# Routed expert tiles: row transposes between the tail down matmuls, half of the tail's low part made earlier, and one weight low part made on GpSimd

## The reference, cut to what matters

```
h = _rmsnorm(x, rms_weight);  topv, topi = top_k(softmax(h @ router_w), 2)
g = einsum('td,edf->tef', ht, w_gate);  u = einsum('td,edf->tef', ht, w_up)
eo = einsum('tef,efd->ted', silu(g) * u, w_down)      # 8 experts, 1024 -> 512 -> 1024
moe = einsum('te,ted->td', w_dense, eo)               # two experts per token
sh = silu(ht @ sw_gate) * (ht @ sw_up) @ sw_down      # shared expert, all tokens
```

## Time and profile before

| what | value |
|---|---|
| median of three runs | 635.94 us |
| span of the profiled execution | 633.0 us |
| TensorE matmul busy | 611.9 us (97%) |
| DVE busy | 524.0 us (83%) |
| ACT busy | 421.6 us (67%) |
| POOL busy | 148.1 us (23%) |
| one routed tile, transposes to transposes | 26.87 us |
| mean granted clock of TensorE | 0.998 |

### The profile page before, as it was taken

The page is one execution under the profiler, slowest core; times in us unless marked ns, Lnnn a source line. Parts: engine busy times, 40 slices in busy tenths (PEclk is TensorE's granted clock), DMA queues, the critical chain, the costliest instruction groups (busy, mean ns, idle before and its releaser), DMA issues.

```text
span 633.0 us, 10577 instructions
## 1 busy us (share of the span) xinstructions
PE 611.9 (97%) x3624; PEld 475.4 (75%) x3625; DVE 524.0 (83%) x886; ACT 421.6 (67%) x558; POOL 148.1 (23%) x167
## 2 busy tenths in 40 slices
PE   8899999998999999999989999999999999999996
PEld 6678888887886444444557888898988989889775
DVE  5888888878787777889999479789797988979686
ACT  4998888889755989784574366639376483855630
POOL 2354446416000333527920310000000000000051
PEclk9999999999999999999999999999999999999999
DMA  8977776765246997936999558796775968759257
GB/s 337 420 291 298 301 303 238 310 267 191 100 174 260 403 362 286 400 134 241 402 364 416 216 204 325 262 370 224 299 315 200 390 210 319 273 219 393 86 176 264
DMA packets 31070, 177.91 MB, mean 281 GB/s; under 512 B 4064, under 2 KB 4064, under 8 KB 14784
## 3 DMA queue, kind: packets, MB, share of 16 engines
q1 hardware_dynamic: 25536, 158.64, 65.3%
q0 software_dynamic: 5504, 18.88, 8.2%
HBM read 154.30 MB, written 23.20 MB: 280 GB/s over the span
## 4 chain that ended last, share of the span: by engine, by line
PE 50%; DVE 19%; ACT 14%; issue 8%; DMA 5%; POOL 2%; DVEq 1%; POOLq 0%; ACTq 0%; SPq 0%
PE BK L2132 10%; PE BK L306 9%; DVE WL L1029 4%; ACT RA L1383 4%; ACT PR L1410 4%; PE BK L2135 3%; PE BK L1882 3%; PE BK L312 3%; PE BK L318 3%; PE BK L313 3%; DMA RA<-wbit 2%; PE BK L2102 2%; PE BK L1827 2%; DMA RX<-wbit 1%; PE BK L2155 1%
## 5 line engine op out<-in xcount | busy, mean ns | idle before, releaser
L2132 PE MATMUL BK<-EX,WH 128*128 128x320 f32 x384 | 101.3, 344 | 0.3
L1029 DVE TENSOR_TENSOR WL<-RA,WH 128x2048 fp32r<-128x2048 f32 x40 | 89.4, 2287 | 7.6 <-ACT WH L1586 7.4
L2135 PE MATMUL BK<-EX,WL 128*128 128x160 f32 x336 | 79.3, 236 | 0.0
L1586 ACT ACTIVATE WH<-RA 128x2048 fp32r<-128x2048 f32 x40 | 73.6, 1910 | 0.2 <-PE BK L1925 0.2
L2132 PEld LDWEIGHTS BK<-EX,WH 128*128 128x128 f32 x384 | 69.7, 188 | 1.9 <-DVE SR L1069 1.9
L2135 PEld LDWEIGHTS BK<-EX,WL 128*128 128x128 f32 x336 | 64.1, 191 | 0.0
L705 POOL DMA_INDIRECT GA<-rows,SLOT x4 | 4.9, 1229 | 240.4 <-DVE WL L1029 239.5
L652 POOL TENSOR_TENSOR HB<-HB,ND (+2 forms) x26 | 28.6, 1121 | 100.5 <-DVE BH L915 99.9
L1482 ACT ACTIVATE RA<-RA,RT 128x2048 int16<-128x2048 f32 x22 | 43.7, 1998 | 3.8 <-DMA RA<-wbit 1.9
L1029 DVE TENSOR_TENSOR WL<-RC,WH 128x2048 fp32r<-128x2048 f32 x20 | 45.0, 2285 | 0.7 <-ACT WH L1586 0.7
L1882 PE MATMUL BK<-TG,XQ 128*128 128x512 bf16 x192 | 42.4, 379 | 0.1
(11 more groups left out here) (328 smaller groups left out, 1644.1 us busy)
## 6 DMA issues: line engine op xcount, KB each, us to landing
RA<-wbit SPq DMA_DIRECT2D x54, 1024.0 KB, 6.7
RA<-wmoe SPq DMA_DIRECT2D x40, 1024.0 KB, 6.5
RC<-wmoe SPq DMA_DIRECT2D x20, 1024.0 KB, 8.0
rows<-ZERO POOLq DMA_DIRECT2D x40, 256.0 KB, 8.2
XG<-rows SPq DMA_DIRECT2D x10, 512.0 KB, 3.7
rows<-YS SPq DMA_DIRECT2D x9, 512.0 KB, 6.0
RA<-wqk SPq DMA_DIRECT2D x7, 640.0 KB, 7.8
RA<-wo SPq DMA_DIRECT2D x4, 1024.0 KB, 7.5
```

Source lines behind the costliest of these rows:

```text
L1029: e.tensor_tensor(WL[m][:, q * RAW:q * RAW + RAW], RC[j][:, :], WH[m][:, q * RAW:q * RAW + RAW].bitcast(f32), ALU.subtract)\
L1586: e.activation(WH[m][:, q * RAW:q * RAW + RAW], RC[2 * m + q][:, :], ACT.Copy)\
L2132: mm = e.matmul(bank[GBK[f]][:, 0:2 * R], WH[m][:, at], EX[:, k, :, :].rearrange("p a b -> p (a b)"), start=k == 0, stop=k == KD - 1)
L2135: e.matmul(bank[GBK[f]][:, 0:R], WL[m][:, at], EX[:, k, 0, :], start=False, stop=False)
```

## The change

Three edits, all in the routed tiles.

1. TensorE: a new helper `tails(h, rows)` does the tail matmuls of two hidden columns (2h and 2h + 1) for both output halves: eight of the sixteen. `tails(0, XG)` now comes straight after the up matmuls, with one of the eight row transposes behind each tail matmul; then the highs; then the lows; `tails(1)` comes last. All waits that stood before and behind the transposes are now ahead of `tails(0, XG)`, except that for `free_c[5]`; a wait for the first `ht_lo` is new.
2. DVE: `routed_hidden_lo` is called once per half. Each call makes the tail's low part for its two columns and then that of the 128 rows. The first call is made between the second and the third piece of `routed_product`.
3. POOL makes WL from the last down chunk RC[5] for experts 2 to 8 and raises `free_c[5]`; DVE makes five low parts per tile in place of six. For the shared expert at the end DVE still makes all six.

The diff:

```diff
--- before.py
+++ after.py
@@ -696,6 +696,10 @@
                                          H3[:, t, :], None).then_inc(s("scat"), 16)
             e.wait_ge(s("scat"), 16 * 2 * NT)
             e.sem_inc(s("rows"), 1)
+            with e.Fori(2, NE + 1) as gi:
+                waits(e, ("m_hi", gi * 6 + 6))
+                at = slice(RAW, 2 * RAW)
+                e.tensor_tensor(WL[2][:, at], RC[5][:, :], WH[2][:, at].bitcast(f32), ALU.subtract).then_inc(free_c[5], 1)
             for j in range(4):
                 e.wait_ge(free_c[j], NE + 2)
             e.wait_ge(s("y_all"), 1)
@@ -1079,16 +1083,14 @@
                     ins = e.tensor_tensor(v, u, v, ALU.add)
                     if n != 1:
                         ins.then_inc(s("eh"), 1)
-
-            def routed_hidden_lo(t):
-                for q in range(2):
-                    ks = slice(2 * q, 2 * q + 2)
-                    e.wait_ge(s("ht_hi"), t * 2 + q + 1)
-                    ins = e.tensor_tensor(HX[:, ks, R + TAIL_R:2 * R], SR[:, ks, 0:P], HX[:, ks, 0:P].bitcast(f32),
-                                          ALU.subtract)
-                    if q == 0:
-                        ins.then_inc(s("ht_lo"), 1)
-                e.tensor_tensor(HX[:, :, R:R + TAIL_R], SR[:, :, P:R], HX[:, :, P:R].bitcast(f32), ALU.subtract)\
+                    else:
+                        routed_hidden_lo(t, 0)
+
+            def routed_hidden_lo(t, q):
+                ks = slice(2 * q, 2 * q + 2)
+                e.wait_ge(s("ht_hi"), t * 2 + q + 1)
+                e.tensor_tensor(HX[:, ks, R:R + TAIL_R], SR[:, ks, P:R], HX[:, ks, P:R].bitcast(f32), ALU.subtract)
+                e.tensor_tensor(HX[:, ks, R + TAIL_R:2 * R], SR[:, ks, 0:P], HX[:, ks, 0:P].bitcast(f32), ALU.subtract)\
                     .then_inc(s("ht_lo"), 1)
 
             def hidden_product(t):
@@ -1275,18 +1277,18 @@
                 gate_sum(t, 1)
                 tail_rows(t + 1)
                 routed_product(t)
-                routed_hidden_lo(t)
+                routed_hidden_lo(t, 1)
                 routed_lo(t + 1)
 
-            def split_all(gi):
+            def split_most(gi):
                 for m in range(3):
-                    split(gi, m)
+                    split(gi, m, (0, 1) if m < 2 else (0,))
             e.wait_ge(s("cnt"), 1)
             with e.Fori(1, NE) as gi:
                 n, t0 = group_of(e, gi)
                 with e.Fori(0, n) as i:
                     tile(t0 + i)
-                split_all(gi + 1)
+                split_most(gi + 1)
             n, t0 = group_of(e, NE)
             with e.Fori(0, n) as i:
                 tile(t0 + i)
@@ -2095,6 +2097,27 @@
                         waits(e, ("ht_hi", 2), (free_c[4], 1), (free_c[5], 1))
                     first_result(n)
 
+            def tails(h, rows=None):
+
+                def row_block(n):
+                    if rows is not None:
+                        m = e.transpose(bank[TB[n // 4]][:, n % 4 * P:n % 4 * P + P], rows[:, n * P:n * P + P], IDF[:, :])
+                        if n % 4 == 3:
+                            m.then_inc(s("et_pe"), 1)
+                for q in range(2):
+                    for k in (2 * h, 2 * h + 1):
+                        n = 4 * q + 2 * (k % 2)
+                        if k:
+                            e.matmul(bank[6 + q][XTAIL, :], HX[:, k, P:R], WL[2][:, down_at(k, q)], start=False, stop=False)
+                            row_block(n)
+                        mm = e.matmul(bank[6 + q][0:2 * TAIL_R, :], HX[:, k, P:R + TAIL_R], WH[2][:, down_at(k, q)],
+                                      start=k == 0, stop=k == KE - 1)
+                        row_block(n if k == 0 else n + 1)
+                        if k == 0:
+                            e.matmul(bank[6 + q][XTAIL, :], HX[:, k, P:R], WL[2][:, down_at(k, q)], start=False, stop=False)
+                            row_block(n + 1)
+                return mm
+
             def gate_halves():
                 for f in range(2):
                     for k in range(KD):
@@ -2137,25 +2160,19 @@
                             mm.then_inc(s("up_pe"), 1)
                         elif f % 2:
                             mm.then_inc(s("gate_pe"), 1)
-                waits(e, ("hsum", t * 5 + 3))
-                routed_rows(t + 1)
-                waits(e, ("ys_a", t + 1), ("ys_d", t + 1), (free_c[4], gi + 1), (free_c[5], gi + 1))
-                for h in range(2):
-                    waits(e, ("ht_hi", t * 2 + h + 1))
-                    for q in range(2):
-                        highs(e, bank[AB[q]], [(HX[:, k, 0:P], WH[2][:, down_at(k, q)], WL[2][:, down_at(k, q)])
-                                               for k in (2 * h, 2 * h + 1)], h == 0)
+                waits(e, ("hsum", t * 5 + 3), ("ht_lo", t * 2 + 1), ("ys_a", t + 1), ("ys_d", t + 1), (free_c[4], gi + 1),
+                      ("e_in", t * 32 + 64))
+                tails(0, XG)
+                for q in range(2):
+                    highs(e, bank[AB[q]], [(HX[:, k, 0:P], WH[2][:, down_at(k, q)], WL[2][:, down_at(k, q)]) for k in (0, 1)])
+                waits(e, ("ht_hi", t * 2 + 2), (free_c[5], gi + 1))
+                for q in range(2):
+                    highs(e, bank[AB[q]], [(HX[:, k, 0:P], WH[2][:, down_at(k, q)], WL[2][:, down_at(k, q)]) for k in (2, 3)],
+                          False)
                 e.wait_ge(s("ht_lo"), t * 2 + 2)
                 for q in range(2):
                     lows(e, bank[AB[q]], [(HX[:, k, R + TAIL_R:2 * R], WH[2][:, down_at(k, q)]) for k in range(KE)])
-                for q in range(2):
-                    for k in range(KE):
-                        if k:
-                            e.matmul(bank[6 + q][XTAIL, :], HX[:, k, P:R], WL[2][:, down_at(k, q)], start=False, stop=False)
-                        mm = e.matmul(bank[6 + q][0:2 * TAIL_R, :], HX[:, k, P:R + TAIL_R], WH[2][:, down_at(k, q)],
-                                      start=k == 0, stop=k == KE - 1)
-                        if k == 0:
-                            e.matmul(bank[6 + q][XTAIL, :], HX[:, k, P:R], WL[2][:, down_at(k, q)], start=False, stop=False)
+                mm = tails(1)
                 mm.then_inc(s("y2_pe"), 1)
 
             def first_result(q):
```

## The result

The changed kernel takes 634.18 us, the median of 10 runs (633.05 to 635.11). The kernel before, run beside it on the same chip, takes 636.11 us (635.15 to 636.66, 10 runs). The ratio is 0.9972, with a 95% interval of 0.9962 to 0.9983: 1.9 us faster. A second measurement gave 633.62 us against 635.99 (ratio 0.9968, 0.9956 to 0.9981).

What follows compares the result with a forecast made beforehand. TensorE's pace bounds the routed stage. Ending its seven `gate_sum(0)` waits (-2.2 us), with 0 for the other two edits, takes the span from 633.0 to 630.8; plus 2.9 gives 633.8 us, range 631.0 to 636.0 (own range 633.0 to 635.0).

Steps and rivals of the forecast that it cites:

- What bounds the stage, and the price of the wait: Routed tiles: TensorE sets the pace; its seven waits of 0.31 us for DVE's `gate_sum(0)` go, -2.2 us.
- DVE's chain: DVE's splits up to `gate_sum(0)`: start 0.9 us later, yet with five splits end 0.9 us before TensorE wants the sum.
- POOL's price: POOL's new subtraction, 4.62 us, takes its turn after DVE's fifth split and delays SP's store some 0.7 us; cost nothing.
- Edit 1: TensorE's 64 row transposes moved between tail matmuls keep their price, 0 us; bounds -3.3 and +1.5.
- Reading (b): Row transposes: streaming 128 plain fp32 columns itself takes 0.108 us, argued from the router's 0.109 us matmuls; no gain.
- The upper bound: Moved transposes: if each of 112 more changes between fp32 and fp32r costs 0.013 us, +1.5 us.
- The estimate of 1.7 us of gain: Moved transposes, by the Trainium skill's 81 ns per load and matmul pair: 64 x (108 - 81) = 1.7 us gained.
- Edit 2 and `ht_lo`: TensorE's new wait for DVE's first low parts before `tails(0)`: cost 0, room 0.1 to 0.3 us, upper bound +1.6.
- rival 2: Nothing gained: `ht_lo` 0.1 us late per tile (+0.8) and type changes (+1.5) offset the ended wait; 636.0 us, chance 0.14.
- Rival 1: Transposes between tail matmuls hide their weight loads, a further -3.3 us; 630.4 us, chance 0.10.
- Rival 3: POOL gets its turn before DVE's fifth split; TensorE waits 3.9 us in seven tiles, +25 us; 661 us, chance 0.08.
- Rival 4: TensorE isn't freed: something else, such as ACT's SR copy, is late at the same place; 635.9 us, chance 0.06.

Runs made afterwards that it cites:

- the GpSimd edit alone: Kernel before with only the sixth low part of experts 2 to 8 moved to POOL, transposes in their old place; 634.07 us, ratio 0.9964.
- the order alone: Changed kernel with all six low-part splits back on DVE, transposes still between tail matmuls; 642.85 us, ratio 1.0108 to the kernel before.

## Why the prediction was right, point by point

- **What bounds the stage, and the price of the wait.** Right. The waits of TensorE went, and with the GpSimd edit alone the stage became 2.18 us shorter, against 7 x 0.31 = 2.2 predicted.
- **DVE's chain.** Right. The first split was to start 0.9 us later in the tile. From the first transpose to it there were 431.50 - 426.76 = 4.74 us, and 433.78 - 428.10 = 5.68 from what stands in that place now: 0.94. `gate_sum(0)` was to end 0.9 us early and ends about 1.0 early. That the 0.9 us by which the chain starts later matters is shown by the order alone, where it costs 6.6 us.
- **POOL's price.** Right: nothing, by the kernel in which nobody does that work. DVE's lead over ACT's sixth copy was to be 0.2 us and is 442.75 - 442.59 = 0.16. POOL's operation ends at 449.34, before DVE's next subtraction or sum with two SBUF inputs, line 1083 at 451.66. The one number that missed is SP's store, put 0.7 us later and in fact 4.0 (447.68 against 451.66). I took the store's time in the earlier trace rows as set by something else, so that a load held until 448.1 would push it only from 447.43. But it follows the end of the second load's issue by 2.1 us in the kernel before and by 1.8 in the changed one, so it moves with the load. Nothing hung on it.
- **Edit 1.** The value was 0 and the measured cost is 64 x 0.004 = 0.26 us; 212.58 - 212.33 = 0.25 by the stages. The stages give edits 1 and 2 together; that it is edit 1 follows from the step of 0.343 us. This is why 1.93 us were gained and not 2.2. Reading (b) held, but my main argument for it was weaker than I thought. The router's matmuls are plain, and each of them runs as two passes, so its 0.109 us is that of a pass. The conclusion survived because a pass of 128 fp32 columns is what a transpose is. Firmer than that argument are the equal steps behind loads of 32, 64 and 128 columns, and the two kernels with plain matmuls. The upper bound, 0.013 us for each of 112 more changes of type, was over five times too high: 0.26 / 112 = 0.002. The estimate of 1.7 us of gain beside it was worked out wrongly, too: it subtracts the price of a pair whose load still counts, and not that of a transpose with its load hidden. There was no gain in any case.
- **Edit 2 and `ht_lo`.** Right in its cost of 0, and by luck in part. I put the room at 0.1 to 0.3 us and said that the queued waits come out of it, without a price for them. From DVE's end to the load it is 0.34 us, and the kernel with the late low part shows that some 0.33 of them are needed. So 0.02 us at most are left, and low parts 0.1 us later would have cost about 8 x 0.1 = 0.8 us, as in rival 2. It is also why that experiment waited 2.0 us a tile where 1.8 were expected. And I priced lateness too low: beyond the wait itself, a large one lowers the clock as well.
- **The sum.** 633.8 against 634.18 and 633.62. The 2.9 us added to the span were not what I took them for, 1.8 of time around it and 1.1 because the profiled run was shorter than the median; they did no harm, since the sum comes out as 635.94 - 2.2 either way. Of the 0.4 us by which 634.18 is more, 0.25 are the cost of edits 1 and 2, and 0.17 are the kernel before, 636.11 in the runs beside it in place of 635.94. The profiled span was to be 630.8 and was 632.3, since the clock ahead of the stage was 0.97; the second profile has 631.3 at 0.999.
- **Rival 1, the loads hide:** fallen. A tail matmul with its transpose takes 0.343 us, not 0.29, whatever the load behind it.
- **Rival 2, nothing gained:** fallen. No wait for line 1093, and 0.25 us of cost in place of 2.3.
- **Rival 3, POOL first:** its mechanism is real and was made to happen. Its wait, 3.9 us predicted, was 3.4 in the kernel made for it; its time, 661 predicted, was 672 there, because each such wait took another 1.6 us, twice some 3, through the clock. The changed kernel keeps clear of it by 0.16 us, in each of its seven tiles.
- **Rival 4, something else late:** fallen, though the GpSimd edit alone shows what DVE itself waits for next, ACT's copy SR, 0.16 us after DVE is free.

## What to carry to other kernels

Moving an operation from VectorE to GpSimd is worth the wait that it ends, here seven times 0.31 us, and not the 2.3 us by which the engine's work shrinks. Find out which of the two engines starts first, since with two SBUF inputs each one stands until the other is done, and price a new wait of TensorE with the clock that it may cost behind it. Measure the room ahead of a wait from the semaphore to the instruction that it releases, the waits queued between them included: here that way took 0.33 of 0.34 us. Judge a change of under 1 us by the length of its stage in the profile, where two executions agreed to 0.05 us here, and not by the span.

## What the runs showed of the hardware beyond that

- A 128x128 fp32 transpose takes 0.108 us in a row and 0.112 between 512-column matmuls. A plain fp32 matmul of the same shape takes 0.221 between them: two passes, each with its own load (128 loads and 128 matmuls for 64 instructions).
- TensorE's granted clock fell to the 1.2 GHz level behind idle stretches of its matmuls of 3.1 us in all seven cases and of 1.75 us in six of eight; it stayed at 1.00 behind stretches of 1.0 us, seven times, in the order alone. Each fall cost 1.55 to 1.6 us, twice 1.2 to 1.4 more. What tells the two tiles without a fall from the six with one was not settled.
- A GpSimd subtraction of 128x2048 fp32 with two SBUF inputs takes 4.46 us of its own here, and its record also holds the time that it stood: 6.51, 6.28 and 6.09 us for the same work. Read its end, and not its length.
